# A graph-attention kernel: masks added to the scores by accumulating DMAs, and a new order of sums and transposes

## The chip, the cores and the metric

The kernel runs on one core of a Trainium2 chip. The metric is the device time of one launch in microseconds; the figure for the kernel before is the median of three runs.

## The reference

```python
# first stage, x [8, 1024, 256], adj [8, 1024, 1024]
h = x @ W.T + b;  ha = h @ attn;  scores = ha @ h.T, -inf where adj == 0
x = layernorm(x + elu(softmax(scores) @ h))
# three graph layers
for l in range(3):
    si = x @ attn_w[l, :256];  sj = x @ attn_w[l, 256:]
    s = si[:, :, None] + sj[:, None, :] + attn_b[l]
    s = where(s >= 0, s, 0.2 * s)
    attn = softmax(where(mask, s, -inf))          # mask: adj with its diagonal
    hh = layernorm(x + attn @ x) * g1[l] + beta1[l]
    x = layernorm(hh + gelu(hh @ W1[l] + b1[l]) @ W2[l] + b2[l]) * g2[l] + beta2[l]
out = layernorm(x1 + x)                            # x1: what went into the layers
```

## The kernel before

The first stage takes some 590 us of the span and isn't touched. It leaves its result in DRAM rows and the mask, as bf16 values to be added to a score (0 or a very large negative number), in a DRAM tensor `mask`. `graph_layers` does the rest, in chunks of 512 rows: 16 chunks a layer, K = 48 in all, and each engine has its own program, a loop over k in an order written out by hand. In iteration k the engines work on the aggregation of chunk k, the feed-forward part of chunk k-1 and the end of chunk k-2, and they make the scores of chunk k+1.

For one chunk the scores lie transposed, in `t`, as NT = 8 tiles j of 128 neighbours by 512 rows. VectorE makes each with one instruction (`score`, L1154) and adds the mask's tile with another (`add_mask`, L1160). The mask's tiles, `maskT`, come by transposing DMAs on SP's queue in two halves (L825), one buffer for all chunks, so SP waits until the chunk before has used a half (L823). ACT makes the exponential twice (`exps`, L1040 as rounded high part `pT_hi`, L1041 in full), VectorE the rest `pT_lo` (`p_lo`, L1166), and PE multiplies them with x (`aggregate`, L1417 to L1419), eight tiles into the PSUM tensor `A`. `exps` may run ahead of PE by the P_RING = 6 buffers of `pT`, and three tiles (LEAD) of the next chunk are done at the end of an iteration.

Then VectorE divides by the sum and adds x (`sums`, L1171 and L1178), takes mean and variance (`stats1`), POOL makes the reciprocal deviation in four small steps (`deviation1`), and ACT normalizes (`n1`, in its step f = 5 and 6). PE transposes the result in the next iteration (`transpose_n1`, L1399, which stands in `aggregate` after tile 1), ACT copies it as `h` and `h_hi` (L1051) and VectorE makes `h_lo` (L1248). PE's `up` (L43 to L45) waits for `h_lo`. The feed-forward loop runs over f = 0 to 7: `up`, the gelu twice on ACT (L1076, L1079), `g_lo` on VectorE (L1253), `down` on PE (L1468 to L1470), with `up` two steps ahead. `stats2`, `deviation2`, `n2` and `scaled` end a chunk; `projections` (or, in the last layer, `final_sum`, `final_stats`, `final_norm`) follow within the f loop of VectorE.

Besides, each row of the attention matrix needs its largest masked neighbour term. `row_top` (L1143) takes it on VectorE from a mask row tile in a ring of three `mask` buffers, which SP loads (L819); of the four tiles of an iteration two stand ahead of `h_lo`, one behind it and one at f = 5. `row_columns` on POOL makes columns of them, which PE turns into rows (`r_rows`).

SP's order in iteration k is: x, the first mask row tile, the store of chunk k-2, both halves of `maskT` of chunk k+2, then the other three mask row tiles. A queue is in order: what stands behind a wait waits too.

Of the kernel before, what the change touches and what calls it, by code (L numbers as in the profile page):

```python
# [17 lines left out]
ALU = mybir.AluOpType  # L18
# [609 lines left out]
def layer_buffers(nc, ctx, x, w1, rows, s_rows, uv):  # L628
# [11 lines left out]
    def sem(name):  # L640
        return ctx.enter_context(nc.semaphore(name))
# [91 lines left out]
    L.s_t = sem("t")  # L733
    L.s_tm = sem("tm")
    L.s_exp = sem("exp")
# [33 lines left out]
def graph_layers(nc, L, x, rows, out, mask, par):  # L769
# [32 lines left out]
    with nc.Block() as block:  # L802
        @block.sync
        def _(sp):
# [16 lines left out]
            def load_maskT(k, half):  # L821
                if k > 0:
                    sp.wait_ge(L.s_tm, NT * (k - 1) + HALF * (half + 1))  # L823
                r = BANK * (k % C)
                sp.dma_start_transpose(L.maskT[:, HALF * half:HALF * (half + 1), :],  # L825
                                       mask_rows[r:r + BANK, BANK * half:BANK * (half + 1)]).then_inc(L.s_maskT[half], 16)
# [82 lines left out]
        def _(pool):  # L909
# [74 lines left out]
            def deviation3(i):  # L984
# [3 lines left out]
                pool.tensor_tensor(L.rstd2[:, :], L.ve2[:, :], L.half[:, :], ALU.pow).then_inc(L.s_fin_rs, 1)  # L988

            v_prepare(0)  # L990
            for part in range(NCH):
                row_columns(0, part)
            v_prepare(1)
            for k in range(K + 2):
                if k >= 2:
                    deviation2(k - 2)
                if k % 2 == 0 and (k + 2) // 2 < NB:
                    for part in range(NCH):
                        row_columns((k + 2) // 2, part)
                for n in rows_made(k):  # L1000
                    v_prepare(n)
                if k < K:
                    deviation1(k)
                if k - 2 >= K - C:
                    deviation3(k - 2 - (K - C))

        @block.scalar
        def _(act):
# [24 lines left out]
            def exps(k, j):  # L1033

                n = NT * k + j
                bias = L.v2[:, k // 2 % VS, j:j + 1]
                act.wait_ge(L.s_tm, n + 1)
                if n >= P_RING:
                    act.wait_ge(L.s_agg, n - P_RING + 1)
                act.activation(L.pT[0][:, n % P_RING, :], L.t[:, j, :], ACT.Exp, bias=bias).then_inc(L.s_exp, 1)  # L1040
                act.activation(L.t[:, j, :], L.t[:, j, :], ACT.Exp, bias=bias).then_inc(L.s_exp, 1)  # L1041
# [92 lines left out]
        def _(dve):  # L1134
# [11 lines left out]
            def score(k, j):  # L1146
# [5 lines left out]
                if k >= 1:  # L1152
                    dve.wait_ge(L.s_lo, n - NT + 1)
                dve.scalar_tensor_tensor(L.t[:, j, :], L.rrow[:, 0, k % 2, :], L.v8[:, k // 2 % VS, j:j + 1], L.rrow[:, 1, k % 2, :],  # L1154
                                         ALU.add, ALU.max).then_inc(L.s_t, 1)

            def add_mask(k, j):
                dve.wait_ge(L.s_t, NT * k + j + 1)
                dve.wait_ge(L.s_maskT[j // HALF], 16 * (k + 1))
                dve.tensor_tensor(L.t[:, j, :], L.t[:, j, :], L.maskT[:, j, :], ALU.add).then_inc(L.s_tm, 1)  # L1160

# [128 lines left out]
            for j in range(NT):  # L1290
                score(0, j)
                add_mask(0, j)
                if j == HALF - 1:
                    for r in range(NT - 2, NT):
                        row_top(r)
# [11 lines left out]
            for k in range(K + 2):  # L1307
# [23 lines left out]
                if ffn and new_layer(k - 1):  # L1331
                    less_b2(layer_of(k - 1))
                for f in range(KF):
                    if ffn:
                        g_lo(k - 1, f)
                    if f == 0 and agg:
                        sums(k)
                    if f == 2 and agg:
                        stats1(k)
                    if f in (1, 3, 5, 7) and projected:  # L1340
                        projections(k - 2, (f // 2,))
                    if after:
                        score(k + 1, f)
                        if f >= 1:
                            add_mask(k + 1, f - 1)
                    if old and not projected:
                        if f == 1:
                            final_sum(k - 2)
                        if f == 3:
                            final_stats(k - 2)  # L1350
                        if f == 6:
                            final_norm(k - 2)
                    if f in (4, 6) and k + 2 < K:
                        x_lo(k + 2, f // 2 - 2)
                    if f == 5:
                        for r in tops[early:]:
                            row_top(r)
                    if f >= 4 and agg and new_layer(k):
                        weights_lo(layer_of(k), f - 4)
                if after:  # L1360
                    add_mask(k + 1, KF - 1)
                if agg and new_layer(k):
# [9 lines left out]
        def _(pe):  # L1372
# [29 lines left out]
            def aggregate(k):  # L1402
# [6 lines left out]
                for j in range(NT):  # L1409
                    n = NT * k + j  # L1410
                    if j == 2 and k >= 1:
                        transpose_n1(k - 1)
                    pe.wait_ge(L.s_lo, n + 1)
# [65 lines left out]
            for k in range(K + 1):  # L1479
                ffn = k >= 1  # L1480
                if k < K:
                    aggregate(k)
                else:
                    transpose_n1(k - 1)
                if ffn and new_layer(k - 1):
# [60 lines left out]
```

## Time and profile before

| | us |
|---|---|
| median of 3 runs (2622.04 to 2627.41) | 2622.75 |
| the profiled execution | 2618.43 |
| its span | 2616.6 |

| engine | busy us | share of the span |
|---|---|---|
| PE | 2385.6 | 91% |
| VectorE (DVE) | 2293.9 | 88% |
| ACT | 1793.4 | 69% |
| POOL | 986.1 | 38% |

The span is the time from the first to the last instruction of one profiled execution; the 1.8 us around it belong to the launch. A row of a group has the idle time of the engine just before its instructions behind a bar, with what ended most of it. In rows in order of time the bracket says how long the engine was idle and what released it. Neighbouring instructions of VectorE and ACT overlap by some 0.1 us in the records, so two in a row take less than the sum of their durations. SPq is SP's queue: its rows are the issues of DMAs, and the landing is the time from an issue to the DMA's semaphore.

### The profile page before, as it was taken

The numbers are of one execution on the slowest core, as the hardware profiler recorded it, in microseconds if no ns is written. First come the engines' busy times: TensorE is split into PE (matmuls) and PEld (weight loads), VectorE is DVE, ScalarE is ACT, GpSimd is POOL, SyncE is SP. The second block draws the span as 40 slices with busy tenths as digits, with TensorE's granted clock in tenths as the row PEclk, the third lists the DMA queues.
The fourth block names the chain that finished last, engine by engine and source line by source line (L and its number), as shares of the span: only waits on it lengthen the run. The fifth ranks groups of instructions, "written<-read, shape, count | busy, mean of one in ns | idle before, by whom it ended". The sixth has DMA issues, their size and how long they took to land.

```text
span 2616.6 us, 46231 instructions
## 1 busy us (share of the span) xinstructions
PE 2385.6 (91%) x16548; PEld 2200.0 (84%) x16548; DVE 2293.9 (88%) x5214; ACT 1793.4 (69%) x2873; POOL 986.1 (38%) x1125
## 2 busy tenths in 40 slices
PE   8999999973899999999899999999989898998996
PEld 6999999963888888888788888988878888888886
DVE  5888888878799999999989999999988999999875
ACT  4444444433777877878778787787777777778774
POOL 4555555544233323323222322432423444443321
PEclk9999999986999999999999999999999999999998
DMA  5444444435323323323232232232333324233221
GB/s 162 123 133 144 144 134 145 142 109 123 97 57 90 89 73 90 87 59 90 85 109 59 80 97 73 81 89 61 86 100 91 79 84 114 70 109 87 47 49 41
DMA packets 349878, 247.34 MB, mean 95 GB/s; under 512 B 214481, under 2 KB 308689, under 8 KB 349649
## 3 DMA queue, kind: packets, MB, share of 16 engines
q1 hardware_dynamic: 349648, 244.39, 33.7%
q8 instruction: 131, 2.15, 0.3%
q14 instruction: 99, 0.80, 0.1%
HBM read 143.68 MB, written 50.33 MB: 74 GB/s over the span
## 4 chain that ended last, share of the span: by engine, by line
DVE 24%; PE 18%; issue 6%; ACT 2%; DMA 0%; POOL 0%; POOLq 0%; SPq 0%; DVEq 0%; ACTq 0%
DVE t L1154 5%; PE A L1417 5%; DVE t L1160 5%; PE A L1418 4%; PE A L1419 4%; DVE g_lo L1253 4%; DVE prod L1224 2%; DVE x_lo L1232 1%; DVE st L1185 1%; DVE spare L1143 1%; DVE u L1178 1%; PE G L1399 1%; PE G L45 1%; ACT g_hi L1079 1%; PE G L43 1%
## 5 line engine op out<-in xcount | busy, mean ns | idle before, releaser
L1417 PE MATMUL A<-x_hi,pT_hi 128*128 128x258 f32 x1536 | 446.0, 290 | 88.3 <-DVE pT_lo L1166 86.7
L1076 ACT ACTIVATE g<-G,b_less 128x512 f32<-128x512 f32 x384 | 264.6, 689 | 380.0 <-PE G L45 375.2
L1468 PE MATMUL Y<-w_hi,g_hi 128*128 128x256 f32 x1536 | 442.5, 288 | 61.2 <-DVE g_lo L1253 59.5
L1418 PE MATMUL A<-x_hi,pT_lo 128*128 128x258 f32 x1536 | 439.0, 286 | 0.0
L1419 PE MATMUL A<-x_lo,pT_hi 128*128 128x256 f32 x1536 | 436.1, 284 | 0.0
L1469 PE MATMUL Y<-w_lo,g_hi 128*128 128x256 f32 x1536 | 428.6, 279 | 0.0
L1470 PE MATMUL Y<-w_hi,g_lo 128*128 128x256 f32 x1536 | 428.2, 279 | 0.0
L1417 PEld LDWEIGHTS A<-x_hi,pT_hi 128*128 128x128 f32 x1536 | 295.6, 192 | 98.2 <-issue 89.4
L1468 PEld LDWEIGHTS Y<-w_hi,g_hi 128*128 128x128 f32 x1536 | 289.4, 188 | 84.5 <-DVE g_lo L1253 74.8
L1253 DVE TENSOR_TENSOR g_lo<-g,g_hi 128x512 fp32r<-128x512 f32 x384 | 264.4, 689 | 106.8 <-ACT g_hi L1079 106.8
L977 POOL TENSOR_TENSOR ve<-mv,eps 128x4 f32<-128x4 f32 x48 | 53.6, 1117 | 711.7 <-DVE mv L1200 711.7
L43 PE MATMUL G<-h_hi,w_hi 128*128 128x512 f32 x768 | 308.2, 401 | 3.5 <-DVE h_lo L1248 3.2
L45 PE MATMUL G<-h_lo,w_hi 128*128 128x512 f32 x768 | 304.9, 397 | 0.0
L44 PE MATMUL G<-h_hi,w_lo 128*128 128x512 f32 x768 | 303.4, 395 | 0.0
L1469 PEld LDWEIGHTS Y<-w_lo,g_hi 128*128 128x128 f32 x1536 | 290.9, 189 | 9.4
L1419 PEld LDWEIGHTS A<-x_lo,pT_hi 128*128 128x128 f32 x1536 | 295.8, 193 | 0.0
L1418 PEld LDWEIGHTS A<-x_hi,pT_lo 128*128 128x128 f32 x1536 | 294.2, 192 | 0.0
L966 POOL TENSOR_TENSOR ve<-mv,eps 128x4 f32<-128x4 f32 x48 | 91.2, 1901 | 528.9 <-DVE mv L1190 528.9
L1154 DVE SCALAR_TENSOR_TENSOR t<-rrow,v 128x512 f32<-128x512 f32 x384 | 286.5, 746 | 4.3 <-ACT rrow L1015 4.3
L1470 PEld LDWEIGHTS Y<-w_hi,g_lo 128*128 128x128 f32 x1536 | 289.8, 189 | 0.0
L1166 DVE TENSOR_TENSOR pT_lo<-t,pT_hi 128x512 fp32r<-128x512 f32 x384 | 247.4, 691 | 37.4 <-ACT t L1041 37.2
L1040 ACT ACTIVATE pT_hi<-t,v 128x512 fp32r<-128x512 f32 x384 | 273.1, 711 | 4.5 <-PE A L1419 2.5
(186 smaller groups left out, 6515.8 us busy)
## 6 DMA issues: line engine op xcount, KB each, us to landing
mask<-mask SPq DMA_DIRECT2D x192, 256.0 KB, 3.9
a_adj_t<-in_adj SPq DMA_DIRECT2D x64, 512.0 KB, 4.1
x_rows<-rows SPq DMA_DIRECT2D x24, 1024.0 KB, 7.2
mask<-a_mask SPq DMA_DIRECT2D x64, 256.0 KB, 4.3
rows<-xo SPq DMA_DIRECT2D x32, 512.0 KB, 2.9
a_xs<-in_x SPq DMA_DIRECT2D x9, 1024.0 KB, 9.9
x_rows<-in_x SPq DMA_DIRECT2D x8, 1024.0 KB, 7.7
rows<-a_xo SPq DMA_DIRECT2D x64, 128.0 KB, 3.7
```

Source lines behind the costliest of these rows:

```text
L43: pe.matmul(out, left_hi, right_hi, start=start, stop=False)
L44: pe.matmul(out, left_lo, right_hi, start=False, stop=False)
L45: return pe.matmul(out, left_hi, right_lo, start=False, stop=stop)
L1040: act.activation(L.pT[0][:, n % P_RING, :], L.t[:, j, :], ACT.Exp, bias=bias).then_inc(L.s_exp, 1)
L1154: dve.scalar_tensor_tensor(L.t[:, j, :], L.rrow[:, 0, k % 2, :], L.v8[:, k // 2 % VS, j:j + 1], L.rrow[:, 1, k % 2, :], ALU.add, ALU.max). ...
L1253: dve.tensor_tensor(L.g_lo[:, n % G_RING, :], L.g[:, n % 2, :], L.g_hi[:, n % G_RING, :].bitcast(F32), ALU.subtract).then_inc(L.s_g_lo, 1)
L1417: pe.matmul(L.A[:, t, 0:DE], hi, L.x_hi[:, par, j, :], start=(j == 0), stop=False)
L1418: pe.matmul(L.A[:, t, 0:DE], lo, L.x_hi[:, par, j, :], start=False, stop=False)
L1419: mm = pe.matmul(L.A[:, t, 0:D], hi, L.x_lo[:, par, j, :], start=False, stop=(j == NT - 1))
L1468: pe.matmul(L.Y[:, t, :], hi, L.w2[0][:, f, :], start=False, stop=False)
L1469: pe.matmul(L.Y[:, t, :], hi, L.w2[1][:, f, :], start=False, stop=False)
L1470: mm = pe.matmul(L.Y[:, t, :], lo, L.w2[0][:, f, :], start=False, stop=last and t % 2 == 1)
```

## The change

VectorE no longer adds the masks. POOL's queue issues four DMAs a chunk, one for each pair of score tiles, from `maskT` (bf16) to `t` (f32) with an accumulating add. Each waits for its two scores and its half of `maskT`, and has a semaphore of its own, for which `exps` and SP's `load_maskT` wait. Group 0 stands in POOL's order before `deviation1`, groups 1 and 2 behind it, group 3 at the end.

On VectorE `sums` moves ahead of the f loop (it was behind `g_lo` 0), `stats1` from f = 2 to 0, the last projections from f = 7 to 6, the second `x_lo` from f = 6 to 5, and the fourth `row_top` from f = 5 to 2 (for k of 1 and up). On PE `transpose_n1` stands ahead of the aggregation.

```diff
--- before.py
+++ after.py
@@ -731,7 +731,7 @@
     L.s_rrowT = sem("rrowT")
     L.s_rrow = sem("rrow")
     L.s_t = sem("t")
-    L.s_tm = sem("tm")
+    L.s_tm = [sem(f"tm{i}") for i in range(4)]
     L.s_exp = sem("exp")
     L.s_lo = sem("lo")
     L.s_agg = sem("agg")
@@ -820,7 +820,8 @@
 
             def load_maskT(k, half):
                 if k > 0:
-                    sp.wait_ge(L.s_tm, NT * (k - 1) + HALF * (half + 1))
+                    for g in range(2 * half, 2 * half + 2):
+                        sp.wait_ge(L.s_tm[g], 16 * k)
                 r = BANK * (k % C)
                 sp.dma_start_transpose(L.maskT[:, HALF * half:HALF * (half + 1), :],
                                        mask_rows[r:r + BANK, BANK * half:BANK * (half + 1)]).then_inc(L.s_maskT[half], 16)
@@ -987,10 +988,17 @@
                 pool.wait_ge(L.s_fin_rs, 2 * i + 1)
                 pool.tensor_tensor(L.rstd2[:, :], L.ve2[:, :], L.half[:, :], ALU.pow).then_inc(L.s_fin_rs, 1)
 
+            def add_masks(k, groups):
+                for g in groups:
+                    pool.wait_ge(L.s_t, NT * k + 2 * g + 2)
+                    pool.wait_ge(L.s_maskT[g // 2], 16 * (k + 1))
+                    pool.dma_start(L.t[:, 2 * g:2 * g + 2, :], L.maskT[:, 2 * g:2 * g + 2, :], accum_op=ALU.add).then_inc(L.s_tm[g], 16)
+
             v_prepare(0)
             for part in range(NCH):
                 row_columns(0, part)
             v_prepare(1)
+            add_masks(0, range(4))
             for k in range(K + 2):
                 if k >= 2:
                     deviation2(k - 2)
@@ -999,10 +1007,16 @@
                         row_columns((k + 2) // 2, part)
                 for n in rows_made(k):
                     v_prepare(n)
+                if k + 1 < K:
+                    add_masks(k + 1, range(1))
                 if k < K:
                     deviation1(k)
+                if k + 1 < K:
+                    add_masks(k + 1, range(1, 3))
                 if k - 2 >= K - C:
                     deviation3(k - 2 - (K - C))
+                if k + 1 < K:
+                    add_masks(k + 1, range(3, 4))
 
         @block.scalar
         def _(act):
@@ -1034,7 +1048,7 @@
 
                 n = NT * k + j
                 bias = L.v2[:, k // 2 % VS, j:j + 1]
-                act.wait_ge(L.s_tm, n + 1)
+                act.wait_ge(L.s_tm[j // 2], 16 * (k + 1))
                 if n >= P_RING:
                     act.wait_ge(L.s_agg, n - P_RING + 1)
                 act.activation(L.pT[0][:, n % P_RING, :], L.t[:, j, :], ACT.Exp, bias=bias).then_inc(L.s_exp, 1)
@@ -1154,11 +1168,6 @@
                 dve.scalar_tensor_tensor(L.t[:, j, :], L.rrow[:, 0, k % 2, :], L.v8[:, k // 2 % VS, j:j + 1], L.rrow[:, 1, k % 2, :],
                                          ALU.add, ALU.max).then_inc(L.s_t, 1)
 
-            def add_mask(k, j):
-                dve.wait_ge(L.s_t, NT * k + j + 1)
-                dve.wait_ge(L.s_maskT[j // HALF], 16 * (k + 1))
-                dve.tensor_tensor(L.t[:, j, :], L.t[:, j, :], L.maskT[:, j, :], ALU.add).then_inc(L.s_tm, 1)
-
             def p_lo(k, j):
                 n = NT * k + j
                 i = n % P_RING
@@ -1289,7 +1298,6 @@
                 row_top(r)
             for j in range(NT):
                 score(0, j)
-                add_mask(0, j)
                 if j == HALF - 1:
                     for r in range(NT - 2, NT):
                         row_top(r)
@@ -1330,19 +1338,17 @@
                     scaled(k - 2)
                 if ffn and new_layer(k - 1):
                     less_b2(layer_of(k - 1))
+                if agg:
+                    sums(k)
                 for f in range(KF):
                     if ffn:
                         g_lo(k - 1, f)
                     if f == 0 and agg:
-                        sums(k)
-                    if f == 2 and agg:
                         stats1(k)
-                    if f in (1, 3, 5, 7) and projected:
-                        projections(k - 2, (f // 2,))
+                    if f in (1, 3, 5, 6) and projected:
+                        projections(k - 2, ((f + 1) // 2 - (f < 6),))
                     if after:
                         score(k + 1, f)
-                        if f >= 1:
-                            add_mask(k + 1, f - 1)
                     if old and not projected:
                         if f == 1:
                             final_sum(k - 2)
@@ -1350,15 +1356,13 @@
                             final_stats(k - 2)
                         if f == 6:
                             final_norm(k - 2)
-                    if f in (4, 6) and k + 2 < K:
-                        x_lo(k + 2, f // 2 - 2)
-                    if f == 5:
+                    if f in (4, 5) and k + 2 < K:
+                        x_lo(k + 2, f - 4)
+                    if f == (2 if k >= 1 else 5):
                         for r in tops[early:]:
                             row_top(r)
                     if f >= 4 and agg and new_layer(k):
                         weights_lo(layer_of(k), f - 4)
-                if after:
-                    add_mask(k + 1, KF - 1)
                 if agg and new_layer(k):
                     weights_lo(layer_of(k), KF - 4)
                 if after:
@@ -1408,8 +1412,6 @@
                 pe.wait_ge(L.s_x_lo, min(k + 2, K) // 2 * 4)
                 for j in range(NT):
                     n = NT * k + j
-                    if j == 2 and k >= 1:
-                        transpose_n1(k - 1)
                     pe.wait_ge(L.s_lo, n + 1)
                     for t in range(TC):
                         ts = slice(t * P, (t + 1) * P)
@@ -1478,10 +1480,10 @@
             v_row(1)
             for k in range(K + 1):
                 ffn = k >= 1
+                if ffn:
+                    transpose_n1(k - 1)
                 if k < K:
                     aggregate(k)
-                else:
-                    transpose_n1(k - 1)
                 if ffn and new_layer(k - 1):
                     fold_b2(layer_of(k - 1))
                 if ffn:
```

## Rows read from the trace of the kernel before

**Rows 1.** a stretch, us, busy PE, PEld, DVE, ACT, POOL (count), PEclk, DMA share, GB/s
```profile
1200.00:1700.00 500.00, 464.79 (x3313) 431.53 (x3312) 461.70 (x1041) 388.06 (x621) 157.87 (x208) 0.99 0.30 82
```

**Rows 2.** who waited for whom: us in total, times, longest
```profile
PE A L1417 <- DVE pT_lo L1166: 86.7, 51, 16.5
PE Y L1468 <- DVE g_lo L1253: 59.5, 55, 3.5
```

**Rows 3.** PE in order of time: start, us, engine, line, tiles, [idle before]
```profile
1407.70 0.40 PE L43 MATMUL G<-h_hi,w_hi 128*128 128x512 f32 x1
...
1412.71 0.28 PE L1468 MATMUL Y<-w_hi,g_hi 128*128 128x256 f32 x1
...
1434.83 0.36 PE L1417 MATMUL A<-x_hi,pT_hi 128*128 128x258 f32 x1 [1.57 <-DVE pT_lo L1166]
...
1447.20 0.40 PE L43 MATMUL G<-h_hi,w_hi 128*128 128x512 f32 x1
```

**Rows 4.** VectorE in order of time, the same chunk
```profile
1410.59 0.69 DVE L1253 TENSOR_TENSOR g_lo<-g,g_hi 128x512 fp32r<-128x512 f32 x1 [1.95 <-ACT g_hi L1079]
...
1411.41 1.66 DVE L1178 SCALAR_TENSOR_TENSOR u<-A,rinv,x_rows 128x256 f32<-128x256 f32 x4
...
1432.80 1.28 DVE L1160 TENSOR_TENSOR t<-t,maskT 128x512 f32<-128x512 f32 x2
...
1441.69 1.21 DVE L1143 CUSTOM_DVE_ANT_0 spare<-vrow,mask 128x1024 bf16<-128x1024 f32 x1
...
1444.28 1.28 DVE L1248 TENSOR_TENSOR h_lo<-h,h_hi 128x512 fp32r<-128x512 f32 x2
...
1447.88 1.23 DVE L1209 TENSOR_TENSOR xo<-xo,be 128x1024 f32<-128x1024 f32 x1
```

**Rows 5.** VectorE in order of time, two chunks of the last layer
```profile
2307.28 0.17 DVE L1171 RECIPROCAL rinv<-A 128x4 f32<-128x4 f32 x1
...
2348.04 0.17 DVE L1171 RECIPROCAL rinv<-A 128x4 f32<-128x4 f32 x1
```

**Rows 6.** groups of VectorE: busy us, mean ns
```profile
L1154 DVE SCALAR_TENSOR_TENSOR t<-rrow,v 128x512 f32<-128x512 f32 x384 | 286.5, 746 | 4.3 <-ACT rrow L1015 4.3
L1160 DVE TENSOR_TENSOR t<-t,maskT 128x512 f32<-128x512 f32 x384 | 260.8, 689 | 0.3
```

**Rows 7.** POOL in order of time
```profile
1418.63 2.08 POOL L966 TENSOR_TENSOR ve<-mv,eps 128x4 f32<-128x4 f32 x1 [11.15 <-DVE mv L1190]
...
1440.73 0.20 POOL L982 TENSOR_TENSOR nmr<-nm,rstd 128x4 f32<-128x4 f32 x1
```

**Rows 8.** ACT in order of time, the same chunk
```profile
1429.09 0.68 ACT L1079 ACTIVATE g_hi<-G,b_less 128x512 fp32r<-128x512 f32 x1
1429.78 1.28 ACT L1040 ACT_TABLE_LOAD   x1
...
1440.91 0.76 ACT L1051 ACTIVATE h<-G,shift,g 128x512 f32<-128x512 f32 x1
```

**Rows 9.** a store's issue, DMA in 40 slices of 1448 to 1452, issues and landings
```profile
1449.13 0.38 SPq L862 DMA_DIRECT2D rows<-xo  x1
...
GB/s 0 0 0 0 0 0 0 0 0 0 0 0 0 0 0 0 0 0 0 0 82 348 348 338 348 338 369 348 348 338 358 338 348 338 358 226 51 20 164 0
...
x_rows<-rows SPq DMA_DIRECT2D x24, 1024.0 KB, 7.2
rows<-xo SPq DMA_DIRECT2D x32, 512.0 KB, 2.9
```

**Rows 10.** SP's queue in order of time, and that mask load's landing
```profile
1434.11 1.89 SPq L825 DMA_TRANSPOSE maskT<-mask  x1
1436.05 0.58 SPq L819 DMA_DIRECT2D mask<-mask  x1
...
DMA to landing us min/median/max: 4.3/4.3/4.3
```
## The prediction

> **What bounds the kernel now.** I read the busy time by stage first. In the graph layers TensorE (PE) and VectorE are both busy some 93% of a stretch, at the full granted clock, 2.4 GHz, so neither can be left out of the sum [rows 1]. Then the waits: PE stands 86.7 us in 51 waits for `pT_lo` before an aggregation, and 59.5 us in 55 waits for `g_lo` before a down product. Of these 146 us one wait alone is 16.5, so 130 us is about all that a faster VectorE can give back [rows 2]. Then one chunk in order of time. I put its zero, T, at the first matmul of up(0), 1407.70; the next one is at 1447.20, so the period is 39.50 us [rows 3]. In it the aggregation starts at T+27.1 after 1.57 us of waiting, because VectorE adds the last two masks until 1434.0 and comes to `pT_lo` only then [rows 3, 4]. Without that wait PE would take 37.9, and the waits for `g_lo` are 1.2 us a chunk on the mean, though less in this one [rows 2]; I put its need at 37.4 us. In the last layer the period is 40.76, since VectorE has the final sum and norm to do in place of projections [rows 5].
>
> **What the change removes.** 384 adds of 689 ns [rows 6]; two in a row take 1.28 us, so each holds VectorE for 0.6 us [rows 4], 8 x 0.6 = 4.8 us a chunk. All of it lies beside PE's work but the part that makes PE late. So if nothing else became late, the most to be had is 39.5 - 37.4 = 2.1 us in each of some 46 chunks, 97 us.
>
> **The new order of the sums.** `sums(k)` now stands ahead of `g_lo(k-1, 0)`. Before, `g_lo` 0 came first, and the sums followed it, ending at 1413.07 [rows 4]. If up(0) starts when `h_lo` ends, VectorE then has a row top and two passes of `scaled` (h_lo ends 1445.5, `scaled` ends 1449.1: 3.6 us), 1.8 us of sums (after the 0.6 of `g_lo`), then 0.6 us of `g_lo`: T+6.0. Down(0) was due at T+5.0 [rows 3, 4]. So this edit costs 1.0 us of PE time in a chunk in which `h_lo` is what PE waits for, and nothing where VectorE is ahead. Its cover before was that h_lo ended 1.7 us before up(0) could start. stats1 at f=0 and the fourth row top at f=2 are moves inside a queue that now has room: free.
>
> **Transposes of n1 ahead of the aggregation.** The same eight matmuls; the copy n1 was finished on ACT long before. They fill PE while the first `pT_lo` is made. Cost nothing, gain up to 0.8 us, not counted, since PE's need stays what it is.
>
> **The DMAs on POOL's queue.** Four a chunk, each reading 256 KB of mask and 512 KB of scores and writing 512 KB. Group 0 waits for score 1, and deviation1 is queued behind it; n1 on ACT follows. VectorE comes to score 1 some 4 us after `g_lo` 0 (stats1, a score, `g_lo` 1, a projection, a score), at about T+10, so deviation1 starts no later than before, at 1418.63, T+10.9 [rows 7]. Groups 1 and 2 have 8 us and more before their exponentials. Group 3 is the one to follow. It waits for score 7, which stands behind `g_lo` 7 and so behind the last gelu: that ended at T+22.07 [rows 8], with the 1.0 us above T+23.1, plus 0.6 for `g_lo` and 0.7 for the score [rows 4, 6] is T+24.4. Call L the time from there until the add's semaphore is up.
>
> No accumulating DMA and no DMA of POOL's queue is in the trace, so L is bounded. The nearest row is a store of 512 KB from SBUF: issued 1449.13, its data at about 348 GB/s from 1450.0 to 1451.6, landing 2.9 us after the issue: 0.9 start, 1.6 data, 0.4 end [rows 9]. Issue on POOL: a four-column operation there takes 0.20 us when VectorE lets it and 2.08 when it doesn't [rows 7]; I take 1.0. Data: if the 768 KB read set it, 2.2 us at that rate; if reads and writes take turns, 1280 KB, 3.7 us. I take the second, since each byte written has first to be read. L = 1.0 + 0.9 + 3.7 + 0.4 = 6.0. Ends: 3.1 (the plain store and 0.2) and 9.3 (the 1024 KB load's 7.2 [rows 9] and 2.1).
>
> The Trainium skill, "DMA: Bandwidth & Descriptors", section on the anatomy of one DMA of the gpsimd path, fits 2.0 us plus bytes over 436 GB/s: 3.2 us for 512 KB, by which L would be at the low end; no run of this kernel shows it yet. "SBUF — State Buffer" (same skill, on contention between the engines' ports) says that a VectorE instruction with two SBUF inputs holds up a GpSimd one that reads SBUF but not one that only writes, and infers that descriptor generation needs only writing. The 0.20 against 2.08 agrees with the first half; by the second my 1.0 for the issue would need no addition.
>
> **Who waits for group 3.** Two chains. The exponentials: the eight pairs take from 1431.06 to 1440.91, 1.23 us each [rows 8], and number 6 is due six pairs after the table load, at about T+31.8, so it is late only when L passes 7.4 us. The other is SP's queue, which is where I expect the bill. `load_maskT(k+2, 1)` must wait until the masks of group 3 are added, and behind it on SP stand the three loads of mask rows for the next row tops. Before, SP issued this transpose at 1434.11, T+26.4, when VectorE had done its last add; now it is T+24.4+L. Its issue takes 1.94 us, and the first mask behind it lands 4.3 us after its own issue [rows 10]. Then VectorE does two row tops (2.6 us, 1441.69 to 1444.28) and the two h_lo (1.2) [rows 4], and up(0) of the next period starts. Before: 26.4+1.9+4.3 = T+32.6, while VectorE reached the row top at T+34.0, so it was hidden. After: 24.4 + 6.0 + 1.9 + 4.3 + 2.6 + 1.2 = 40.4 us a period, 34.4 + L, against 39.5: +0.9. PE's own work no longer matters to it.
>
> **The sum.** 31 periods of the first two layers at +0.9: +28. Ten of the third: score 7 slips by 0.5 behind the final norm (POOL makes its deviation between groups 2 and 3), 40.9 against 40.76 [rows 5]: +1.4. Layer changes, the start and the last three chunks, where no row tops are left, gain from the lighter VectorE, up to 10, I take 5. Sum +24. The profiled execution took 2618.43 us, 1.8 outside its span of 2616.6; so 2643. The median of the runs is 4.3 above it: 2647. The same sum is nought at a period of 39.8, L = 5.4.
>
> **Rivals.** (A) The adds are quick, L under 5.3. The transposes go out early, and once L is under 4.3 the mask rows land before VectorE needs them. Then the period is set by ACT and VectorE: last gelu T+23.1, table load and eight pairs 11.2 us (1429.78 to 1440.91) [rows 8], `pT_lo` 0.6, row tops and `h_lo` 3.8: 38.7; PE 37.4 + 1.0 = 38.4. That is -0.8 x 31 - 1.5 x 10 - 5 = -45, 2578, and 2562 if the sums cost nothing. Faster. For it: the DMA engines are idle 70% of the time [rows 1], and transfers of 512 KB without arithmetic land in 2.9. Against it: the issue by software, and two reads where the store has one. The page's fit above would give this case. (B) The accumulate is slow, or its descriptors are made slowly beside VectorE, L = 9.3: 43.7 a period, +4.2 x 31 + 3.4 x 10 - 5 = +159, 2782. (C) L within 0.1 of 5.4: the chain on SP takes the place of the one on VectorE, and nothing is left of the gain, 2623. That the change doesn't do what it says is not likely: the adds do leave VectorE.
>
> **How the numbers follow.** Forecast (L from 5.5 to 8) 0.42, A 0.36, B 0.14, C 0.08. Slower by over 0.2% (5 us, about what a measurement of this kernel can tell from none) 0.56, within it 0.08, faster 0.36. The range reaches over all of A, to 2562, and to L = 8 (42.4 a period, +2.9 x 31 + 2.1 x 10 - 5 = +106, some 2730 and a little over for the landings, which vary): 2735. The forecast's own range is 2627 to 2735.
>
> **What would show it.** Right: VectorE's idle time before the row tops ends with `mask<-mask` DMAs in most chunks, SP's waits for the transposes name the accumulating DMA, up(0) waits for h_lo, and the wait of the aggregation for `pT_lo` is gone. L is to be read as the time from issue to landing of `t<-maskT`. Wrong: an L under 5.4; or VectorE never idle for a mask, with a period under 39; or exponentials waiting for the add, which would make L over 7.4. The sums' 1.0 us is seen as PE's wait for `g_lo` before the first down product.

## The result, and the profile after

| | before | after |
|---|---|---|
| median of 7 runs, us | 2622.04 (2615.34 to 2627.41) | 2604.84 (2594.40 to 2612.43) |
| span of the profiled execution, us | 2616.6 | 2608.7 |

The ratio is 0.9935 (0.9916 to 0.9953): 17 us faster, where 2647, 25 us slower, was forecast. The time lies in the stated range, and the sign is the other one. The traces below are of one execution each, 2618.43 us before and 2610.52 after, so they differ by 7.9 us and not by 17.

The page of the changed kernel, with the masks' DMAs as a queue of their own (q0) and in the list of issues (KB each, median us to landing):

```profile
span 2608.7 us, 45941 instructions
PE 2408.8 (92%) x16548; PEld 2208.3 (85%) x16548; DVE 2087.6 (80%) x4830; ACT 1789.6 (69%) x2873; POOL 1030.0 (39%) x1317
...
q0 software_dynamic: 27648, 100.68, 16.3%
...
t<-maskT POOLq DMA_DIRECT2D x192, 512.0 KB, 4.0
```

VectorE lost 206 us of its 2294. PE waits elsewhere now. The waits of the changed kernel (us in total, times, longest), and under them the one on SP's queue:

```profile
ACT g L1090 <- DVE g_lo L1262: 53.5, 33, 1.9
PE G L43 <- DVE h_lo L1257: 59.0, 42, 4.1
DVE spare L1157 <- DMA mask<-mask: 37.6, 27, 2.9
PE Y L1470 <- DVE g_lo L1262: 28.2, 42, 2.6
PE A L1419 <- DVE pT_lo L1175: 20.1, 11, 7.1
ACT pT_hi L1054 <- DMA t<-maskT: 21.5, 6, 15.2
```

```profile
SPq L824 <- DMA t<-maskT: 789.5, 76, 23.8
```

Against [rows 2]: the 86.7 us for `pT_lo` are 20.1, and the 59.5 for `g_lo` are 28.2, but 59.0 us for `h_lo` have come, and VectorE stands 37.6 us for mask rows. ACT's gelu waits 53.5 us for `g_lo`; before the change no such wait is among the large ones. The stretch that answers to [rows 1] shows VectorE at 82% instead of 92% and PE at 94 instead of 93, with the DMA share up from 0.30 to 0.53:

```profile
1200.00:1700.00 500.00, 470.10 (x3290) 432.33 (x3288) 408.99 (x939) 387.06 (x618) 179.83 (x260) 0.98 0.53 133
```

One chunk in which the adds make nobody late, from up(0) to up(0), in order of time (the landing line is that of the add issued at 1397.08, group 3's):

```profile
1373.02 0.50 PE L43 MATMUL G<-h_hi,w_hi 128*128 128x512 f32 x1 [0.54 <-DVE h_lo L1257]
...
1396.04 0.74 DVE L1168 SCALAR_TENSOR_TENSOR t<-rrow,v 128x512 f32<-128x512 f32 x1
...
1397.08 0.86 POOL L995 DMA_DIRECT2D t<-maskT  x1 [3.96 <-DVE t L1168]
DMA to landing us min/median/max: 5.0/5.0/5.0
...
1402.10 2.05 SPq L826 DMA_TRANSPOSE maskT<-mask  x1
1404.21 0.57 SPq L819 DMA_DIRECT2D mask<-mask  x1
...
1407.28 1.22 DVE L1157 CUSTOM_DVE_ANT_0 spare<-vrow,mask 128x1024 bf16<-128x1024 f32 x1
...
1409.80 1.29 DVE L1257 TENSOR_TENSOR h_lo<-h,h_hi 128x512 fp32r<-128x512 f32 x2
...
1411.14 0.50 PE L43 MATMUL G<-h_hi,w_hi 128*128 128x512 f32 x1 [0.43 <-DVE h_lo L1257]
...
1417.07 0.39 PE L1470 MATMUL Y<-w_hi,g_hi 128*128 128x256 f32 x1 [0.63 <-DVE g_lo L1262]
```

The period is 1411.14 - 1373.02 = 38.12 us, against 39.50 in [rows 3]. The rows of [rows 4, 8, 10] are all here in their new places: score 7 ends at T+23.8, POOL issues the add 0.3 us later, it lands 5.0 us after its issue, SP's transpose goes out at 1402.10, mask row loads follow, and the row tops start without a wait. Then come `h_lo` and PE's wait of 0.43 us for it. The links add up to the period even here: 23.8 + 5.3 + 2.2 + 3.0 + 3.8 = 38.1 us (score, add, transpose, landing of the mask row, row tops and `h_lo`). The last row is the first down product, 0.63 us late for `g_lo`, which is the price of the sums.

A chunk in which the adds took longer (the landing line is that of the add issued at 827.92):

```profile
822.90 3.71 SPq L826 DMA_TRANSPOSE maskT<-mask  x1
...
823.10 0.85 POOL L995 DMA_DIRECT2D t<-maskT  x1 [3.25 <-DVE t L1168]
827.92 0.86 POOL L995 DMA_DIRECT2D t<-maskT  x1 [3.96 <-DVE t L1168]
DMA to landing us min/median/max: 8.3/8.3/8.3
...
834.30 0.72 ACT L1054 ACTIVATE pT_hi<-t,v 128x512 fp32r<-128x512 f32 x1 [1.73 <-DMA t<-maskT]
...
836.25 2.13 SPq L826 DMA_TRANSPOSE maskT<-mask  x1
838.43 0.57 SPq L819 DMA_DIRECT2D mask<-mask  x1
...
841.40 1.23 DVE L1157 CUSTOM_DVE_ANT_0 spare<-vrow,mask 128x1024 bf16<-128x1024 f32 x1 [1.36 <-DMA mask<-mask]
...
845.27 0.50 PE L43 MATMUL G<-h_hi,w_hi 128*128 128x512 f32 x1 [2.85 <-DVE h_lo L1257]
```

SP's transpose of half 0 went out at 822.90 and group 2's add 0.2 us behind it. That add took 11.2 us to land and group 3's 8.3 us. The exponentials waited 1.73 us for group 2's, the second transpose left at 836.25 behind group 3's, VectorE waited 1.36 us for the mask row behind it, and PE 2.85 us for `h_lo`. From reciprocal to reciprocal this chunk took 41.36 us. In the last layer it is group 3's add that meets the transpose of half 0: the store of the finished rows stands ahead of the transposes on SP and waits for the final norm. One such transpose went out at 2084.52 and group 3's add at 2085.57; the add took 7.0 us, and group 2's, issued at 2079.90, took 3.8.

Where the time went, by the starts of the reciprocal of `sums`, one in each chunk:

| stretch | before | after |
|---|---|---|
| 14 periods of the first layer | 722.72 to 1276.11, 39.53 each | 729.58 to 1280.60, 39.36 each |
| 14 periods of the second | 1371.66 to 1924.96, 39.52 each | 1376.45 to 1925.71, 39.23 each |
| 8 periods of the last | 2062.76 to 2388.80, 40.76 each | 2062.20 to 2393.08, 41.36 each |
| last 4 chunks, with no row tops left | 2388.80 to 2550.98, 162.2 | 2393.08 to 2541.80, 148.7 |

So the first layers gain 2 to 4 us each, the last one loses 5, and the end, where no chunk waits for mask rows any more, gains 13.5. The start loses 6.9 us (722.72 against 729.58), nearly all of it before the first aggregation:

```profile
614.10 3.75 POOL L995 DMA_DIRECT2D t<-maskT  x4
...
618.26 0.72 ACT L1054 ACTIVATE pT_hi<-t,v 128x512 fp32r<-128x512 f32 x1 [15.21 <-DMA t<-maskT]
```

The four adds of chunk 0 stand in POOL's order behind the second `v_prepare`, which ends at 614.1, though their scores are there by 610.1. ACT's first exponential waits 15.21 us for them, and the first aggregation starts at 622.75 instead of 616.28. No kernel with these adds ahead of the second `v_prepare` was run.

### The profile page after: what moved, and what is told of

Read it like the earlier page. It is cut to its first block and busy times, and to the rows that moved or that the text cites. A ratio compares the mean times of both kernels' runs of the same rounds, so it can differ in the third digit from the quotient of the medians.

```text
span 2608.7 us, 45941 instructions
## 1 busy us (share of the span) xinstructions
PE 2408.8 (92%) x16548; PEld 2208.3 (85%) x16548; DVE 2087.6 (80%) x4830; ACT 1789.6 (69%) x2873; POOL 1030.0 (39%) x1317
## 5 line engine op out<-in xcount | busy, mean ns | idle before, releaser
L995 POOL DMA_DIRECT2D t<-maskT x192 | 172.7, 910 | 840.6 <-DVE t L1168 824.4
L1419 PE MATMUL A<-x_hi,pT_hi 128*128 128x258 f32 x1536 | 445.8, 290 | 25.8 <-DVE pT_lo L1175 20.1
L1470 PE MATMUL Y<-w_hi,g_hi 128*128 128x256 f32 x1536 | 440.0, 286 | 28.2 <-DVE g_lo L1262 28.2
L1175 DVE TENSOR_TENSOR pT_lo<-t,pT_hi 128x512 fp32r<-128x512 f32 x384 | 260.3, 687 | 187.5 <-ACT t L1055 187.5
L43 PE MATMUL G<-h_hi,w_hi 128*128 128x512 f32 x768 | 320.3, 417 | 59.3 <-DVE h_lo L1257 59.0
L45 PE MATMUL G<-h_lo,w_hi 128*128 128x512 f32 x768 | 311.8, 406 | 0.0
L44 PE MATMUL G<-h_hi,w_lo 128*128 128x512 f32 x768 | 310.8, 405 | 0.0
L1157 DVE CUSTOM_DVE_ANT_0 spare<-vrow,mask 128x1024 bf16<-128x1024 f32 x192 | 234.4, 1221 | 52.3 <-DMA mask<-mask 37.6
```

Source lines behind the costliest of these rows:

```text
L43: pe.matmul(out, left_hi, right_hi, start=start, stop=False)
L44: pe.matmul(out, left_lo, right_hi, start=False, stop=False)
L45: return pe.matmul(out, left_hi, right_lo, start=False, stop=stop)
L1419: pe.matmul(L.A[:, t, 0:DE], hi, L.x_hi[:, par, j, :], start=(j == 0), stop=False)
L1470: pe.matmul(L.Y[:, t, :], hi, L.w2[0][:, f, :], start=False, stop=False)
```

## The experiments

Theory 1 is the prediction's chain: group 3's add, the transpose of half 1, the mask rows behind it on SP, row tops, `h_lo`, up(0). Theory 2: the exponentials themselves wait for long adds. Theory 3: the new order of VectorE's work is what eats the gain. All ratios are against the kernel before on the same chip, whose medians were 2621.6 to 2622.9 us.

**Mask rows ahead of the transposes on SP**

```diff
+                for r in tops[1:]:
+                    load_mask(r + MASKS)
                 if k + 2 < K:
                     for half in range(2):
                         load_maskT(k + 2, half)
-                for r in tops[1:]:
-                    load_mask(r + MASKS)
```

> SP issues the three mask row loads of an iteration ahead of the two transposes instead of behind them; everything else is the changed kernel. Theory 1 (the chain on SP: group 3's add, transpose of half 1, mask rows, row tops, h_lo sets the period): VectorE's waits for mask rows (37.6 us in 27) vanish, the periods of 39.4 (first two layers) and 41.4 us (last layer) come down to the 38.1 that the quiet chunks already show, and to some 39 in the last layer: 30 x 1.2 + 9 x 2.3 = 57 us less, near 2550. Theory 2 (what costs is that the exponentials themselves wait for adds that take 6 to 8 us beside a transpose): chunks with such an add stay at 41, gain under 15 us, 2590 to 2600. Theory 3 (the new order of the sums is what eats the gain): no change, 2605.

Measured: 2570.97 us, ratio 0.9807 (0.9793 to 0.9820), 34 us under the changed kernel. The waits:

```profile
PE Y L1470 <- DVE g_lo L1262: 35.2, 55, 2.3
PE G L43 <- DVE h_lo L1257: 27.8, 41, 3.2
PE A L1419 <- DVE pT_lo L1175: 26.8, 9, 6.4
```

The wait for mask rows is no longer among the sixty longest, and the one for `h_lo` fell from 59.0 to 27.8. Periods of the first two layers are 38.10 and 38.88 in turn with hardly an exception, those of the last layer 38.7 to 40.2 but for one of 44.5. Theory 1 stands. Theory 2 doesn't explain the gain: group 2's adds still take up to 9.1 us in the first two layers, and no period there shows it. It explains one chunk: in the last layer an add took 13.5 us, an exponential waited 7.3 us for it, and that is the period of 44.5. The rest to the 2550 expected is for the most part the alternation with 38.88, which Theory 3 has to account for.

**Both transposes behind all four adds**

```diff
-                    for g in range(2 * half, 2 * half + 2):
+                    for g in range(4):
                         sp.wait_ge(L.s_tm[g], 16 * k)
```

> Both transposes wait for all four adds, so none is in flight beside groups 2 and 3; the order on SP is that of the changed kernel. All theories: the adds of groups 2 and 3 land in 3.9 us throughout (now up to 11). Theory 1: the mask rows then stand behind two transposes instead of one, 1.9 us later and some more for the landing, so a period is 24.4 + 4.0 + 2 x 1.9 + 4.3 to 5.6 + 3.8 = 40.3 to 41.6: slower than the changed kernel, 2625 to 2660. Theory 2: the exponentials never wait, the periods go to 38.1 and the time to about 2560.

Measured: 2654.57 us, 1.0114 (1.0097 to 1.0131): slower than both kernels, in the range that Theory 1 gave. Adds land in 3.9 us (median; group 3's of the last layer too, at the median, against 6.1 in the changed kernel), so those were long because a transpose was in flight beside them; but the mask rows now stand behind two transposes:

```profile
PE G L43 <- DVE h_lo L1257: 99.6, 42, 4.7
DVE spare L1157 <- DMA mask<-mask: 79.2, 43, 4.4
```

**Both edits together**

> Both edits: mask rows ahead of the transposes on SP, and both transposes behind all four adds. Theory 1: about the first experiment's time, near 2550, or some 5 us under it where a long add made ACT late. Theory 2: clearly under the first experiment, by 20 us or more. Theory 3: 2605.

Measured: 2565.83 us, 0.9785 (0.9772 to 0.9798), 5 us under the first experiment, about what its period of 44.5 was too long. In the first two layers the adds are short again and the periods are the same 38.10 and 38.88 in turn, so long adds cost nothing there once the mask rows don't stand behind them. Theory 2 is out as the main cause. A transpose is not the only DMA that makes an add long: in the last layer here three mask row loads go out around group 3's add, and it takes 6.5 to 8.0 us.

**Sums back behind g_lo 0**

```diff
-                if agg:
-                    sums(k)
                 for f in range(KF):
                     if ffn:
                         g_lo(k - 1, f)
                     if f == 0 and agg:
+                        sums(k)
                         stats1(k)
```

> Only the sums go back behind g_lo 0 (stats1 stays at f = 0); the rest is the changed kernel. The prediction's step says that sums ahead of g_lo cost PE 1.0 us in a chunk in which PE waits for h_lo. If so PE's waits for g_lo (28.2 us in 42) nearly vanish and the time falls by 0.6 to 1.0 us x 42, to 2565 to 2580 (Theory 3 is then at least a part). If the order costs nothing: 2605, as the changed kernel.

Measured: 2593.34 us, 0.9896 (0.9875 to 0.9917), 11.5 us under the changed kernel, less than expected. PE's waits for `g_lo` were 23.9 us in 32 instead of 28.2 in 42. Quiet periods were 38.10 for both parities, as they should be, but VectorE still stood 36.9 us for mask rows. What is left of the waits for `g_lo` is about what stats1 at f = 0 causes by itself (below: 25.1 us in 28). The profiled execution of this kernel was 10 us above its median.

**The same on top of both edits on SP**

> The third experiment's kernel (mask rows first on SP, transposes behind all four adds) with the sums back behind g_lo 0. That kernel's periods alternate between 38.10 and 38.88, and PE still waits 34 us in 53 for g_lo; the fourth experiment's quiet chunks show 38.10 for both parities. Theory 1 with the step on the sums right: all quiet periods 38.1, PE's waits for g_lo under 20 us, 2566 - 16 x 0.8 - some in the last layer, 2545 to 2556. If the sums' place matters only beside late masks: 2566.

Measured: 2553.45 us, 0.9741 (0.9727 to 0.9754), 12 us under 2565.83, in the expected range. Nearly every period of the first two layers is 38.10.

**The adds by DMA alone, all orders as before the change**

> The masks are added by POOL's DMAs, but sums, stats1, projections, x_lo, the fourth row top and the transposes of n1 stand where they stood before the change. Theory 1: the chain on SP is there as in the changed kernel, sums cost nothing, PE idles up to 0.8 us more a chunk before the aggregation: 2593 (sums back) to 2625, middle 2605. A rival, that the order is what made the adds worth their while: 2640 or more.

The edit takes back every hunk of the change on VectorE and PE but the removal of `add_mask`, and keeps the ones on SP, POOL and ACT. Measured: 2542.78 us, 0.9697 (0.9684 to 0.9711): 79 us faster than before, and 62 faster than the changed kernel. That is outside everything I had written down for it. The waits:

```profile
PE A L1421 <- DVE pT_lo L1175: 50.7, 46, 15.0
DVE spare L1157 <- DMA mask<-mask: 26.0, 25, 2.5
PE G L43 <- DVE h_lo L1257: 18.3, 16, 3.2
PE Y L1472 <- DVE g_lo L1262: 12.8, 11, 3.1
```

ACT's waits for `g_lo` are down to one of 0.9 us, PE's are 12.8 us in 11. Quiet periods are 37.1 and 38.0 in turn, and in each PE has one stop left, 0.72 us for `pT_lo`. So PE's own work is some 36.4 and 37.2 us.

**The order alone, with the adds on VectorE**

> VectorE adds the masks as before the change; sums, stats1, projections, x_lo, fourth row top and transposes stand in the new order. VectorE is idle 107 us in 62 before g_lo before the change; sums ahead of g_lo 0 fill that, so its masks are done 1 to 1.9 us earlier, and the transposes fill what PE waits for pT_lo. Theory 1: this half gives most of the changed kernel's gain, 1.0 us a period, 2575 to 2590, and the adds' DMAs as placed give nothing on top or cost. Rival: the order by itself changes nothing or loses the 1.0 us of g_lo, 2620 to 2650, and the gain comes from VectorE's relief.

Measured: 2566.42 us, 0.9790 (0.9777 to 0.9803): 55 us faster than before, a little more than expected. What PE waits for is now mostly `g_lo`:

```profile
PE Y L1466 <- DVE g_lo L1253: 56.9, 71, 2.3
PE A L1415 <- DVE pT_lo L1166: 20.6, 7, 7.6
```

The two halves together give 17 us, alone 79 and 55. Quiet periods show how they overlap. Before, PE stood 1.6 us for `pT_lo` in each, and 0.4 and 0.9 us in turn for `g_lo`. With the adds alone 0.72 us for `pT_lo` is left. With the order alone the wait for `pT_lo` is gone and 0.5 and 1.5 us in turn for `g_lo` are there. With both it is 0.6 to 0.7 for `g_lo` and 0.45 for `h_lo`, 1.1 us. So both shorten the wait for `pT_lo`, one by taking 4.8 us off VectorE, the other by putting the sums into VectorE's idle time before `g_lo` 0 [rows 4] and the transposes ahead of the aggregation. On top of the adds the order has 0.72 us to give and costs 1.1, before any late mask row.

**The kernel before with mask rows ahead of the transposes**

> The kernel before with only SP's order changed: mask rows ahead of the two transposes. Its mask rows land at T+32.6 and VectorE comes to them at T+34.0, so Theory 1 expects no change, 2622 within 0.3%. If an earlier mask row helps by itself, the first experiment's gain would not be the chain of the adds: 2590 to 2610.

Measured: 2620.09 us, 0.9993 (0.9984 to 1.0002). No change: before, the chain on SP was covered, as the prediction said.

**The order, one piece at a time, on the adds alone (2542.78)**

Mask rows ahead of the transposes:

> The sixth experiment's kernel (adds by DMA, old order: 2543 us) with the mask rows ahead of the transposes on SP. Its VectorE still waits 26 us in 25 for mask rows and PE 18 us for h_lo. If the chain on SP is all that is left of the adds' price, those go and the time falls by 10 to 20 us, 2523 to 2535. If PE's own 37.05 us a period already is the limit there: 2540.

2528.96 us, 0.9642 (0.9627 to 0.9657): 14 less, in the expected range. What is left is the wait for `pT_lo`, one of which is 14.9 us at the start:

```profile
PE A L1421 <- DVE pT_lo L1175: 50.4, 43, 14.9
PE G L43 <- DVE h_lo L1257: 6.6, 9, 3.2
```

Transposes of n1 ahead of the aggregation:

```diff
...
-                    if j == 2 and k >= 1:
-                        transpose_n1(k - 1)
...
+                if ffn:
+                    transpose_n1(k - 1)
                 if k < K:
                     aggregate(k)
-                else:
-                    transpose_n1(k - 1)
```

> The sixth experiment's kernel with the transposes of n1 ahead of the aggregation and nothing else of the new order. PE's wait of 0.72 us for pT_lo before each aggregation is filled; the prediction called this edit free. 2525 to 2543. If this edit is what costs the changed kernel its 62 us against the sixth: 2570 or more.

2555.44 us, 0.9734 (0.9710 to 0.9757): 13 more, neither free nor the 27 and more of a main cause. The wait moved from `pT_lo` to `h_lo`:

```profile
PE G L43 <- DVE h_lo L1257: 49.4, 42, 3.9
PE A L1419 <- DVE pT_lo L1175: 17.4, 7, 6.5
```

stats1 at f = 0, behind the sums:

```diff
                     if f == 0 and agg:
                         sums(k)
-                    if f == 2 and agg:
                         stats1(k)
```

> The sixth experiment's kernel with stats1 at f = 0, right behind the sums, and nothing else of the new order. The prediction called this move free. If 1.7 us of stats1 ahead of g_lo 1 make PE wait, g_lo waits grow by 0.6 to 1.0 us a chunk and the time goes to 2560 to 2580; if it is free, 2543.

2568.22 us, 0.9790 (0.9771 to 0.9810): 25 more. ACT waits for `g_lo`:

```profile
ACT g L1090 <- DVE g_lo L1262: 71.3, 53, 1.9
```

Sums ahead of g_lo 0, stats1 left at f = 2:

```diff
+                if agg:
+                    sums(k)
                 for f in range(KF):
                     if ffn:
                         g_lo(k - 1, f)
-                    if f == 0 and agg:
-                        sums(k)
```

> The sixth experiment's kernel with the sums ahead of g_lo 0, stats1 left at f = 2, and nothing else of the new order. The prediction's step on the sums: 1.0 us where PE waits for h_lo, which in that kernel is every other chunk: 2555 to 2575. If free: 2543.

2573.82 us, 0.9823 (0.9803 to 0.9843): 31 more, the same way:

```profile
ACT g L1090 <- DVE g_lo L1262: 66.0, 40, 1.9
```

The three pieces sum to 69 us, against the 62 between the adds alone and the changed kernel. That they add up so nearly is partly chance: the sums cost 31 us here and only 12 on top of the rest of the new order (the fourth and fifth experiments). (The moves of the last projections, of `x_lo` and of the fourth row top were not tried by themselves.)

**What the DMA costs, piece by piece**

The changed kernel's DMA without the accumulate, with the cast from bf16 to f32 (names shortened in this cut):

```diff
-pool.dma_start(L.t[...], L.maskT[...], accum_op=ALU.add)
+pool.dma_start(L.t[...], L.maskT[...])
```

> The changed kernel with the same DMAs from POOL's queue, 256 KB of bf16 mask to 512 KB of f32, but without the accumulate: they overwrite the scores, so the scores are left out of the softmax and the time is that of a kernel that computes something else. My L took 3.7 us for data because of the second read. If reading the destination costs, the quiet landings fall from 3.9 to about 3 us, and the ones beside a transpose from 6 to 11 to under 6. If the accumulate is free, 3.9 stays, and the price is that of the queue and of 512 KB written.

```profile
t<-maskT POOLq DMA_DIRECT2D x192, 512.0 KB, 3.0
```

And as a plain copy to a bf16 buffer (`L.dump`, three slots of two tiles, a DMA into the first of which also waits for the last one there):

> The changed kernel with POOL's DMAs as plain copies of the mask, 256 KB bf16 to a bf16 buffer that nobody reads: the masks are left out of the scores, so the result is that of unmasked attention in these layers. It gives the fixed part of a DMA of POOL's queue: 2.5 to 3 us if bytes and accumulate make up the rest of the 3.9, 3.5 or more if the queue itself is the price.

```profile
dump<-maskT POOLq DMA_DIRECT2D x192, 256.0 KB, 2.3
```

Landing medians are 2.3 us for 256 KB copied, 3.0 with 512 KB written by the cast, and with the accumulate 4.0 in the changed kernel and 3.9 where nothing runs beside it. The time of one run each was 2567.90 (cast) and 2556.24 (copy), 37 and 49 under the changed kernel with the rest in its order. VectorE's waits for mask rows were 13.8 and 8.4 us, against 37.6: the shorter L, the less the chain on SP binds.

**The three good edits together**

Adds by DMA, old order on VectorE, mask rows first on SP, transposes first on PE:

> Adds by DMA, old order on VectorE, mask rows ahead of the transposes on SP (2529 us), and the transposes of n1 ahead of the aggregation. With late mask rows that last edit cost 13 us, nearly all in the last layer, and PE's waits only moved from pT_lo to h_lo (49 us). If what it cost was the chain of the mask rows, it now gains: PE's 50 us of waits for pT_lo shrink, 2510 to 2525. If it costs by itself (exponentials held by the ring of pT, which PE empties 0.9 us later): 2535 to 2545.

Measured: 2524.13 us, 0.9625 (0.9611 to 0.9638), 5 us under the same kernel without the transposes' move and 81 under the changed one.

```profile
PE G L43 <- DVE h_lo L1257: 24.6, 42, 3.2
PE A L1419 <- DVE pT_lo L1175: 19.6, 8, 6.6
```

So that move costs only beside late mask rows, and gains a little without them. PE is busy 94% of this span of 2523.2 us. The 6.5 us lost at the start are in this kernel too: its first exponential waits as long.

## Why the prediction was wrong

**What bounds the kernel, and the most to be had.** Right in kind. PE's need was put at 37.4 us a period; the quiet periods of four kernels show 36.4 to 37.8 without their waits. Of the 97 us to be had the adds alone gave 79 and the last kernel 98. That the last figure agrees so well is partly luck, since it has the end's gain in it, which was no part of the 97.

**The step that failed: the length of the chain on SP, and in it L.** The forecast had this chain bind every period, at 34.4 + L with L = 6.0. The terms, and their means read from the trace of the changed kernel (14 periods each of the first two layers, 9 of the last, from up(0) to up(0)):

| us | forecast | first two layers | last layer |
|---|---|---|---|
| score 7 ends, from up(0) | 24.4 | 24.26 | 25.06 |
| L | 6.0 | 5.12 | 6.52 |
| from there to the first mask row's issue | 1.9 | 2.09 | 2.13 |
| its landing | 4.3 | 3.45 | 3.52 |
| two row tops, `h_lo`, up(0) | 3.8 | 3.92 | 4.09 |
| sum | 40.4 | 38.84 | 41.32 |
| period | 40.4 | 39.29 | 41.31 |

In the first two layers L was 0.9 too long and the rest 0.7. With the measured values the chain lies under the old period of 39.5, and it bound in only 10 of the 28 periods, those in which VectorE stood for a mask row; they took 40.1 on the mean, the others 38.8. That turned +28 us in these layers into -6.4, and with it the sign. Neither error alone turns it: the forecast's L with the measured rest gives 39.7, the measured L with the forecast's rest 39.5, both about the period before.

**L.** For an undisturbed add it was 4.2: 0.3 from the score to the issue and 3.9 to the landing. The term that was off is the data, 3.7, chosen because reads and writes were thought to take turns. The accumulate adds 0.9 us to the cast's 3.0. Issue to landing of the plain store was 2.9 [rows 9], and that row was nearer than the sum I preferred. And L isn't constant. Group 3's add took over 5.5 us in 20 of 47 chunks, 5.2 on the mean, because the transpose of half 0 is released by group 1's add, goes out just when group 2 does, and makes both late; in the last layer it goes out just ahead of group 3. I had looked at the two transposes as things that wait, and not as traffic. In the last layer this made L longer than forecast, 6.5. It also made group 2's add 11.2 us long, so an exponential did wait for an add, and not for group 3's, the one that I had followed.

**The chain on SP.** Right in its links. In the disturbed chunk 23.8 + 8.6 + 2.2 + 3.0 + 3.8 = 41.4 (up(0) 803.87 to 845.27, 41.40). The mask row's landing was put at 4.3 from one row [rows 10], which was near that kernel's median of 4.1, but in the changed kernel the median is 3.3. In the quiet chunks the floor of rival A, 38.7, was 38.1 and 38.9 in turn. That the chain costs time is shown by three kernels: rows first, 34 us less; transposes later, 50 more; the kernel before with rows first, nothing.

**The order of the sums.** The mechanism was nearly right: 1.0 us where `h_lo` binds, measured 0.63 of PE's waiting in the quiet chunk, and 31 us in all on the adds alone, some 0.75 a chunk (12 us on top of the rest of the new order). It reaches further than written, since `g` has two buffers and the third gelu waits for `g_lo` 0: 66 us in 40 on ACT.

**The moves called free.** Wrong. stats1 at f = 0 puts 1.7 us ahead of `g_lo` 1 and costs 25 us; room in a queue over a whole iteration is not room ahead of the one instruction that others wait for. The transposes cost 13 beside late mask rows. Together the new order costs 62 us on top of the adds alone; my sum had some 40 x 1.0 us of it inside its 40.4.

**The sum.** Start, layer changes and the last chunks were put into a lump of 5 us of gain. The last chunks gave 13.5 by themselves, and the start lost 6.9, since the first adds stand behind other work of POOL. The last layer was forecast at 40.9 and came to 41.3 by the table, for another reason than written: L.

**The sign.** The forecast was a small difference of two large terms (some 80 us of gain against the chain and the order), with L near its break-even. Rival A had the sign and gave 2578; its condition, L under 5.3, held in about half the chunks and in none of the last layer's, and the time ended between the two. Nothing in the experiments speaks against the two-term account, but how much of the first experiment's 34 us is the clock's (below) was not separated.

The Trainium skill's fit ("DMA: Bandwidth & Descriptors", on the anatomy of one DMA of the gpsimd path), 3.2 us for 512 KB, lies between this case's 3.0 without and 3.9 with the accumulate.

## What to carry to other kernels

When work moves from an engine to a DMA, ask first what stands on the issuing queues behind the wait for its end: here one reordering of two loads on SP was worth 34 us, more than the whole change. Try a move of work and a new order apart: each of these gained by itself (79 and 55 us), and together they gave 17, since both paid for the same wait. Between two candidates for the same slot, look at the one instruction that others wait for (`g_lo`), not at the queue's mean load.

## What the runs showed of the hardware

Accumulating DMAs on POOL's queue land in 3.9 us for 512 KB when alone. One that was issued 0.2 us behind a transposing DMA took 11.2 us, and the next, issued 5.0 us behind it, 8.3; one issued 1.6 us behind a transpose (864.34 and 865.91) took 4.7. POOL itself is held 0.86 to 0.94 us by the issue (medians of the four groups). Without the accumulate the longest landing of a group 2 in the first two layers was 5.5 us, against 11.2.

The granted clock of PE fell after this long wait and not after the short one of the next chunk. The changed kernel around the disturbed chunk (us, then busy time of PE, PEld, DVE, ACT, POOL with counts, granted clock, DMA share, GB/s):

```profile
842.00:845.00 3.00, 0.41 (x4) 0.20 (x2) 2.86 (x6) 2.98 (x5) 0.00 (x0) 1.00 0.42 115
845.00:848.00 3.00, 2.73 (x8) 2.21 (x9) 2.97 (x5) 0.53 (x2) 0.00 (x0) 0.68 0.02 5
848.00:851.00 3.00, 3.00 (x15) 2.47 (x15) 2.96 (x7) 1.90 (x4) 0.00 (x0) 0.75 0.42 148
851.00:854.00 3.00, 3.00 (x20) 2.70 (x20) 3.00 (x12) 2.00 (x4) 0.00 (x0) 1.00 0.08 26
```

PE worked 0.41 of 3 us, stood 2.85 us for `h_lo`, and the next two stretches were granted 0.68 and 0.75 of 2.4 GHz, part of each at the lower level, 1.2 GHz. By these shares 3 x 0.32 + 3 x 0.25 = 1.7 us of full speed were lost, an estimate. The period behind it took 39.55 us (845.27 to 884.82) against 38.86 of a quiet one of the same parity, and score 7 in it came at T+25.2 instead of T+24.5, so 0.7 of them reached the time. After the wait of 0.47 us of the next chunk the clock stayed at full, and so it did after one of 2.2 us at 1083.02, behind which score 7 came at T+24.5:

```profile
884.00:888.00 4.00, 3.53 (x18) 2.77 (x18) 3.97 (x6) 3.41 (x6) 3.84 (x6) 1.00 0.20 72
...
1083.00:1086.00 3.00, 2.98 (x14) 2.44 (x15) 2.96 (x4) 1.27 (x2) 0.00 (x0) 1.00 0.00 0
```

So a long wait of PE can cost more than its own length, as this one did. Over the span the granted clock was 0.974 before, 0.966 after, 0.978 with mask rows first, and 0.958 with the transposes late. One minus the clock, times the span, is an estimate of the full speed withheld: 68, 89, 57 and 111 us. Between the changed kernel and mask rows first it falls by 32 us while the spans differ by 39. How much of it is in the time is not shown; in the chunk above it was 0.7 of 1.7.
